# A sorting loop in which GpSimd takes four small operations from VectorE, and VectorE tests a later pair's blocks in between

## What is computed

```
messages = x[dst] @ W_msg + b_msg
msg_sum  = segment_sum(messages, src, 12500)
counts   = segment_sum(ones, src, 12500)
h_agg    = msg_sum / maximum(counts, 1)
h        = concatenate([x @ W_lin + b_lin, h_agg], axis=1) @ W_upd + b_upd
out      = layernorm(x + relu(h))
```

## Time and profile before

| | us |
|---|---|
| three runs | 1266.48, 1282.43, 1290.02 |
| their median | 1282.43 |
| the profiled execution | 1267.35 |
| its span in the trace | 1265.6 |

### The profile page before, as it was taken

The page is one execution under the profiler, slowest core; times in us unless marked ns, Lnnn a source line. Parts: engine busy times, 40 slices in busy tenths (PEclk is TensorE's granted clock), DMA queues, the critical chain, the costliest instruction groups (busy, mean ns, idle before and its releaser), DMA issues. The chain is left out here.

```text
span 1265.6 us, 51991 instructions
## 1 busy us (share of the span) xinstructions
PE 1083.6 (86%) x21321; PEld 965.2 (76%) x21321; DVE 942.5 (74%) x2190; ACT 769.3 (61%) x1827; POOL 522.7 (41%) x502
## 2 busy tenths in 40 slices
PE   1939889888697499998988889998999899999996
PEld 0939889887687387887778777877877778888785
DVE  7999999999999756666665666665665556666674
ACT  0313333331111398888877777887887778888885
POOL 3000000000000477666665655665665556666660
PEclk9969989989898699999999998999999999999998
DMA  8212322311340434444444433443444344444430
GB/s 112 80 54 90 117 94 101 106 66 31 111 121 3 118 86 115 105 105 101 104 101 100 103 84 76 101 100 83 104 101 98 95 100 104 104 104 103 104 77 14
DMA packets 121290, 116.27 MB, mean 92 GB/s; under 512 B 35291, under 2 KB 103896, under 8 KB 120983
## 3 DMA queue, kind: packets, MB, share of 16 engines
q1 hardware_dynamic: 95548, 64.96, 19.4%
q0 software_dynamic: 23024, 47.31, 16.4%
q10 hardware_dynamic: 2490, 0.67, 0.3%
HBM read 89.79 MB, written 23.10 MB: 89 GB/s over the span
## 5 line engine op out<-in xcount | busy, mean ns | idle before, releaser
L1286 PE MATMUL slot<-big 32*128 32x384 bf16 x7925 | 744.7, 327 | 53.6 <-issue 29.5
L567 ACT ACTIVATE big<-slot 128x384 bf16<-128x384 f32 x1600 | 666.6, 496 | 147.3 <-PE slot L1286 126.4
L1299 PE MATMUL acc<-big 32*128 32x385 bf16 x6400 | 710.4, 328 | 10.6 <-issue 8.9
L1286 PEld LDWEIGHTS slot<-big 32*128 32x128 bf16 x7925 | 475.7, 93 | 107.7 <-ACT big L567 32.9
L633 POOL DMA_INDIRECT big<-x,dst_at x400 | 425.8, 1064 | 268.2 <-PE acc L1312 176.9
L1299 PEld LDWEIGHTS acc<-big 32*128 32x128 bf16 x6400 | 438.6, 94 | 46.5 <-issue 25.2
L1312 PE MATMUL acc<-big 32*128 32x385 bf16 x1600 | 358.0, 328 | 0.0
L955 DVE TENSOR_TENSOR big<-col_lo,iota_lo 128x512 bf16<-128x512 f16 x400 | 149.9, 416 | 238.9 <-PE acc L1299 237.0
L1324 PE MATMUL acc<-big 32*128 32x385 bf16 x600 | 196.3, 327 | 5.1 <-issue 5.1
L627 POOL MEMSET big<- 128x8 bf16 x4 | 0.2, 100 | 410.3 <-issue 410.3
L943 DVE TENSOR_SCALAR big<-big,iota_k 128x2048 bf16<-128x2048 f16 (+8 forms) x225 | 155.1, 718 | 1.2 <-issue 1.2
(11 more groups left out here) (150 smaller groups left out, 830.7 us busy)
## 6 DMA issues: line engine op xcount, KB each, us to landing
big<-rows SPq DMA_DIRECT2D x100, 128.0 KB
big<-in_x SPq DMA_DIRECT2D x48, 256.0 KB, 3.0
x<-big SPq DMA_DIRECT2D x24, 384.0 KB, 2.6
big<-x,dst_at POOLq DMA_INDIRECT x400
base<-big SPq DMA_DIRECT2D x24, 256.0 KB, 2.5
big<-base SPq DMA_DIRECT2D x24, 256.0 KB
out<-big SPq DMA_DIRECT2D x24, 256.0 KB
big<-x SPq DMA_DIRECT2D x8, 168.0 KB, 2.9
```

Source lines behind the costliest of these rows:

```text
L567: act.activation(xg[R % NX][:, i, 0:F3], slot[i // 2][:, i % 2, 0:F3], ACT.Copy).then_inc(s["xg_ready"], 1)
L1286: ins = nc.tensor.matmul(slot[lane // 2][:, lane % 2, 0:F3], W[q % NW_][rows, hot_at(g, k), :], xwin[rows, WIN_AT[g] + k, :], start=k == 0 ...
L1299: ins = nc.tensor.matmul(acc[lane][:, 0:F3 + 1], l_of(R, i)[rows, :], xg[R % NX][rows, i, 0:F3 + 1], start=r == 0 and i == 0, stop=last an ...
```

## The change

The four small operations of `route` move from DVE to POOL, in a new function `find_slots`. The two that made `sbb` and `val` are rewritten: `sbb` becomes the larger of the comparison and 1/512, which gives 1 or 1/512 as before, so that `val` is a plain product. `route` is split: `take_ranks` (the reduction) and the rest, with `test_hi(u+2)` between the two. DVE's comparison with the slots now waits for POOL (`slots_known`). After the loop the maximum over all ranks comes before `route(39)`.

```diff
+            def find_slots(u):
+
+                k2 = two_chunks(r_all, u)
+                pool.wait_ge(s["ranks_taken"], u + 1)
+                if u > 0:
+                    pool.wait_ge(s["route_ready"], u)
+                nc.gpsimd.tensor_scalar(col(s32), k2, SL - 0.5, -float(SL), ALU.is_gt, ALU.mult).then_inc(s["pool_made"], 1)
+                nc.gpsimd.tensor_scalar(col(sbb), k2, SL - 0.5, 1.0 / 512.0, ALU.is_gt, ALU.max).then_inc(s["pool_made"], 1)
+                pool.wait_ge(s["pool_made"], 2 * u + 2)
+                nc.gpsimd.tensor_tensor(col(s16), k2, col(s32), ALU.add)
+                nc.gpsimd.tensor_tensor(val[0:EP, :, :], sbb[0:EP, :].unsqueeze(1).to_broadcast([EP, 2, 2 * T]), nodes[0:EP, u, :, :],
+                                        ALU.mult).then_inc(s["slots_known"], 1)
...
+            def take_ranks(u):
+                dve.wait_ge(s["Q_added"], u + 1)
+                with nc.allow_low_precision("whole numbers below 2521 in fp16; 64 and over are told apart"):
+                    nc.vector.tensor_reduce(two_chunks(r_all, u), Q_ps[u % 2].rearrange("p (a h j) -> p a j h", h=NH, j=2), AX.X, ALU.add).then_inc(s["ranks_taken"], 1)
+
             def route(u):
 
                 b = u % 2
...
-                k0 = mark(nc.vector.tensor_scalar(col(s32), k2, SL - 0.5, -float(SL), ALU.is_gt, ALU.mult))
-                k1 = mark(nc.vector.tensor_scalar(col(sbb), k2, SL - 0.5, 511.0 / 512.0, ALU.is_gt, ALU.mult))
-                after(k0)
-                k0 = mark(nc.vector.tensor_tensor(col(s16), k2, col(s32), ALU.add))
-                after(k1)
-                k1 = mark(nc.vector.scalar_tensor_tensor(out=val[0:EP, :, :], in0=sbb[0:EP, :].unsqueeze(1).to_broadcast([EP, 2, 2 * T]), scalar=1.0 / 512.0,
-                                                         in1=nodes[0:EP, u, :, :], op0=ALU.add, op1=ALU.mult))
-                after(k0)
+                dve.wait_ge(s["slots_known"], u + 1)
                 if u > 0:
                     dve.wait_ge(s["route_ready"], u)
...
                 if u > 0:
-                    route(u - 1)
+                    take_ranks(u - 1)
                 if u + 2 < U:
                     test_hi(u + 2)
+                if u > 0:
+                    route(u - 1)
                 if u < XB:
                     split_1(u)
...
+            take_ranks(U - 1)
+            dve.wait_ge(s["ranks_taken"], U)
+            nc.vector.reduce_max(flag4[0:EP, 1:2], r_all[0:EP, :, :].rearrange("p c t -> p (c t)"), AX.X)
             route(U - 1)
-            nc.vector.reduce_max(flag4[0:EP, 1:2], r_all[0:EP, :, :].rearrange("p c t -> p (c t)"), AX.X)
```

More of the change, by code:

```diff
@@ L251, in gnn_program @@
                  "flag_ready flag_summed flag_known rows_ready wT_made wT_taken w_made w_taken dve_made edges_ready "
-                 "x_turned xT_taken base_made base_taken constant_added hi_cast r1_made mid_cast lo_made OH_ready R_made R_taken Q_made Q_added ranks_taken route_ready T_made T_taken decoded lo_ready lo_laid lo_taken dm_ready sv_made spills_ready "
+                 "x_turned xT_taken base_made base_taken constant_added hi_cast r1_made mid_cast lo_made OH_ready R_made R_taken Q_made Q_added ranks_taken pool_made slots_known route_ready T_made T_taken decoded lo_ready lo_laid lo_taken dm_ready sv_made spills_ready "
                  "rows_stored wins_loaded numbers_ready rare_ready rare_loaded W_ready L_ready Ld_ready Lsp_ready xg_ready ones_set "
@@ L306, in two_chunks, with col @@
             return a[0:EP, 2 * u:2 * u + 2, :].rearrange("p c (a j) -> p (c a) j", j=2)
+        def col(a):
+            return a[0:EP, :].rearrange("p (a j) -> p a j", j=2)
         def bc(a, n):
@@ L613, in _ @@
                            .rearrange("p (a f) -> p a f", f=F3)).then_inc(s["pads_stored"], 16)
+            def find_slots(u):
[9 more added lines that the diff above has]
+                                        ALU.mult).then_inc(s["slots_known"], 1)
+            pool.wait_ge(s["edges_ready"], 1)
+            for u in range(U):
+                if u == CS // 2:
+                    pool.wait_ge(s["edges_ready"], 2)
+                find_slots(u)
             pool.wait_ge(s["flag_known"], 1)
```

## The result

The changed kernel takes 1313.2 us (median of four runs, 1310.8 to 1315.7); the kernel before 1282.4 (four runs beside them). The two medians stand in the ratio 1.024; the ratio of fast executions alone, with slower ones of the kernel before left out, is 1.035, with a 95% interval of 1.029 to 1.040. So the change is slower by 3.5%, outside 2%, and the time itself is near the 1312 us forecast. The profiled execution took 1310.8 us, 43 us more than that of the kernel before (1267.4).

A forecast was written before the change was run, and what follows sets the result against it. DVE was taken to bound the sorting. 37 x (c - 0.58), 2 x (c - 0.32) and 1.26 us sum to 39c - 20.8, +29.5 us with c = 1.29; 1282.4 + 29.5 = 1312 us, range 1270 to 1345.

The forecast's parts named there:

- The blocking: Sorting loop: POOL's first read waits until test_hi has read its inputs; c - 0.58 = 0.71 us lost a pair.
- The chain c: POOL's four small operations with its wait for itself and the signal to DVE: 1.29 us a pair.
- The short chain: Rival in the sorting loop: blocked, but POOL's time goes with columns; c = 0.87 us, +13 us, 1296 us; chance 0.27.
- Pairs 37 and 38: Last two loop iterations, no test left: the pairs wait openly for POOL, 2 x (c - 0.32) us lost.
- What I had at nothing: Sorting loop: POOL's other waits, the earlier test_hi, and more PE idling or lower clock were to cost nothing.
- my own signs of being wrong: Prediction wrong if c is under 1.0 or over 2, POOL gets its reads in, or DVE waits for lower-clock PE.
- that term: Behind the loop: the maximum over the ranks now stands before pair 39's comparison, 2.11 instead of 0.85 us; 1.26 us lost.
- The total: Whole kernel: the loss of 29.5 us carried over to the median of 1282.4 us gives 1312 us.
- the sum: Sorting stage: covered pairs, two open pairs and loop end together 39c - 20.8, +29.5 us with c = 1.29.
- No blocking: Rival in the sorting loop: test_hi leaves POOL its reads and covers the chain; -18 us, 1264 us; chance 0.19.
- the slow chain: Rival: POOL operations over 0.5 us each, c passes 2.15 us, loss 63 us, up to 153 us (1435); chance 0.07.

The follow-up runs named there:

- e3_one_input: Changed kernel with test_hi back behind route and an unused one-input maximum between reduction and comparison; 1348 us, ratio 1.063 to the kernel before.
- e4_two_inputs: Changed kernel with test_hi back behind route and done a second time between reduction and comparison; 1385.5 us, ratio 1.093 to the kernel before.
- e1_dve_order: Changed kernel with the four small operations back on DVE behind test_hi, POOL idle; ratio 1.0015 to the kernel before.
- e9_act_first: Changed kernel with ScalarE making the factor before copying the next counts, two small operations on DVE, POOL idle, old loop end; ratio 0.997 to the kernel before.
- e5_dve_order_tail: e1_dve_order with the maximum over all ranks back behind route(39); ratio 1.007 to the kernel before.
- e10_five_blocks: e5_dve_order_tail with five OH buffers in place of four; ratio 1.003 to the kernel before.

## Why the prediction was right

**The blocking** was right, by its own signs: POOL's first test ends 0.22 us after `test_hi`, the comparison has an idle time released by POOL (1.31 us; "about 1.2" was said), and the iteration takes 9.58 us (the comparison at 189.57 and again at 199.15), where 9.46 was said. That POOL is blocked and not merely slow is shown by the covers of e3_one_input and e4_two_inputs (0.35 against 2.27 us for the same operation). The reason given, that both inputs of `test_hi` are in SBUF, fits all runs but is not isolated by them.

**The chain c** was 1.29 us and measured 1.39 (from 186.03 + 2.15 to 189.57). The four operations take 0.35, 0.35, 0.26 and 0.34 us, not 0.29 each, and start up to 0.43 us after each other. The short chain, in which time goes with columns, fell here: a test of 40 columns takes longer than the select of 128. Between the two-input operations the columns do show: 80 take 0.08 us more than 40, or 2.0 ns a column, in fp16. The Trainium skill, page "GPSIMD Engine Reference", section "3.1 Elementwise — side-by-side cycle accounting", has 4497 ns for 2048 columns of a two-input operation in fp32; the estimate from it, 2.2 ns a column, agrees. By 2.0 ns a column the 40 columns of the sum make 0.08 of its 0.26 us; the rest would be fixed cost. A loss of 0.81 us in place of 0.71 for 37 pairs is 3.7 us of the difference between 29.5 and 37.6.

**Pairs 37 and 38** cost 1.90 us from the reduction to the comparison, against 0.85, as 0.36 + 0.17 + 1.29 = 1.82 had it.

**What I had at nothing, and was not:** TensorE. I wrote that it has room, that its lower clock costs nothing and that the earlier `test_hi` costs nothing, since its buffer was freed one `fill_bins` ago. One of my own signs of being wrong, that TensorE at its lower clock becomes what DVE waits for, came true in these places. The granted clock over the sorting fell from 0.92 to 0.86, and at the end the last `fill_bins`, now behind 4.90 us of idling, took 3.65 us. From the last reduction to the third stage it is 2.9 us more (20.25 against 17.34) in place of the 1.26 of that term: the term's own part was right (443.07 - 440.95 = 2.12 us, where 2.11 was said), and 1.6 us came on top. In the loop the early test waited five times for a `fill_bins` that was late. But these 7.0 us are no loss of that size, as the timeline of one shows:

```profile
407.56 0.36 DVE L823 TENSOR_REDUCE big<-acc 125x40 f16<-125x200 f32 x1
...
408.01 0.35 POOL L624 TENSOR_SCALAR big<-big 125x40 f16<-125x40 f16 x1 [5.04 <-DVE big L823]
...
409.32 2.24 DVE L794 TENSOR_TENSOR big<-big 125x4000 f16<-125x4000 f16 x1 [1.40 <-PE acc L1214]
411.48 0.82 DVE L831 TENSOR_TENSOR big<-big 125x1280 f16<-125x1280 f16 x1
```

While the test waits, POOL does its chain undisturbed, and the comparison comes 3.92 us after the reduction, 0.1 later than in the blocked pairs. Two waits take the same place. The sum is then: 37 x 0.81 = 30.0, the two pairs 2.1, the end 2.9, the five late tests 0.5, `pick` 1.3 more than before: 36.8, against 37.6 measured, of which 0.3 lie before the first reduction.

**The total** was carried from the profiled execution to the median, and that held: 1312 forecast, 1313.2 measured. In part it is luck. Against the 1282.4 us from which I started, the forecast is a ratio of 1.023, and it lies below the measured interval of 1.029 to 1.040: the sorting stage lost 37.6 us where the sum had 29.5. The medians are only 30.8 apart, and the four runs of the kernel before spread over 24 us. In the later comparisons its median was 1272.7, 1274.8 and 1277.9 us (17, 17 and 11 runs), and the changed kernel took 1302.2 in the one run beside the second of them. The direction and the mechanism don't depend on that.

**The rivals.** "No blocking" fell with the 2.27 us, and the slow chain with operations of 0.26 to 0.35 us. The arithmetic of "no blocking" would probably have erred too: e1_dve_order saved 6 us in the pairs and e9_act_first 13, and little of either was left at the end of sorting, so a part of its 18 us would have gone the same way. That part I had not priced.

## What to carry to other kernels

Before work goes to GpSimd "under" a VectorE operation, look at which operation that is: this 125x4000 comparison with two inputs in SBUF shut GpSimd's read out for its whole length (2.27 us for an operation of 0.35), and the handed-over chain lay behind it, not under it. A reduction with one SBUF input did hide the chain, and ScalarE was not held up beside the same comparison (0.32 and 0.23 us). Other operations with one input need a look in a trace of their own. When an engine is busy 98% of a stage and another has 0.65 us of room an iteration, savings on the first are soon paid back in waits for the second: so it went in e1_dve_order, e5_dve_order_tail, e9_act_first and e10_five_blocks.

## What the hardware showed that I had not expected

Small operations on GpSimd are long for their size: 0.35 us for a test of 125x40, with 0.43 us from one start to the next, where VectorE takes 0.17 us and starts another after 0.08. The exclusion works in both directions and by order of arrival, but not with equal weight. A GpSimd product that came 0.05 us behind a two-input comparison took 0.97 us in place of 0.34 and ended 0.20 us after it, so it was held up until the comparison was done. When it began 0.07 us ahead, it ran undisturbed, and the comparison took 0.13 us longer, though the product still had 0.27 us to go. The prediction took it that whichever comes second is blocked fully; that holds here for GpSimd as the second and not in full for VectorE.
